# The last convolution's taps on column halves of TensorE with stacked tokens, and reordered steps in the first and third convolution and the last feed-forward part

## The reference

```python
y = conv_depthwise_3x3(x); y = y * inv + shift; return einsum('bchw,oc->bohw', y, w_pw)
...
diag = (q * k).sum(-1) * SCALE
m0_sum = diag.sum()
ktv = einsum('bnd,bne->bde', k, v)
out = m0_sum * v + SCALE * einsum('bnd,bde->bne', q, ktv) - diag[..., None] * v
```

## Time and profile before

| | |
|---|---|
| median of 3 runs | 1213.68 us (1210.94 to 1234.04) |
| the profiled execution | 1208.81 us, span 1207.0 us |
| mean granted TensorE clock | 0.952 |
| TensorE busy | 1111.6 us, 92% |
| VectorE busy | 810.0 us, 67% |
| ScalarE busy | 485.6 us, 40% |
| GpSimd busy | 255.7 us, 21% |

### The profile page before, as it was taken

One profiled execution on the slowest core, in us unless ns is written; L12 is line 12 of the kernel. 1 busy time (PEld: TensorE's weight loads), 2 busy tenths in 40 slices (PEclk: granted clock), 3 DMA queues, 4 the chain that ended last, 5 costly groups with the idle time before them and its releaser, 6 DMA issues. The chain is left out here.

```text
span 1207.0 us, 24782 instructions
## 1 busy us (share of the span) xinstructions
PE 1111.6 (92%) x8774; PEld 967.2 (80%) x8774; DVE 810.0 (67%) x2904; ACT 485.6 (40%) x976; POOL 255.7 (21%) x244
## 2 busy tenths in 40 slices
PE   3979999989999999999998988889999999999776
PEld 3758999978899998899997666568999987887554
DVE  7257676756766664577776767655877767776775
ACT  3843433425555553343342324233343422332451
POOL 5013212110211000212122534342121221211110
PEclk9979999988999999899999789899999999999887
DMA  4302010010000000000001121200000000000001
GB/s 148 95 5 69 22 47 5 0 53 1 2 2 2 1 2 1 1 2 1 0 0 36 37 48 25 49 1 1 2 1 0 0 1 1 2 1 1 5 10 40
DMA packets 15246, 21.60 MB, mean 18 GB/s; under 512 B 8761, under 2 KB 10383, under 8 KB 15026
## 3 DMA queue, kind: packets, MB, share of 16 engines
q1 hardware_dynamic: 14434, 18.53, 5.2%
q10 hardware_dynamic: 720, 1.85, 0.4%
HBM read 11.59 MB, written 3.15 MB: 12 GB/s over the span
## 5 line engine op out<-in xcount | busy, mean ns | idle before, releaser
L1222 PEld LDWEIGHTS moe_dn<-all_w,moe_hid 128*128 128x128 f32 x2304 | 269.7, 192 | 6.8 <-DVEq L1116 1.5
L1222 PE MATMUL moe_dn<-all_w,moe_hid 128*128 128x96 f32 x2304 | 271.9, 275 | 1.1 <-DVEq L1116 1.1
L1163 ACT ACTIVATE moe_hid<-moe_up 128x512 f32<-128x512 f32 x288 | 169.5, 598 | 234.5 <-PE moe_up L1214 221.4
L1212 PE MATMUL moe_up<-front_xh,front_w1h 97*128 97x512 f32 x288 | 122.1, 424 | 0.6 <-PEq L1708 0.3
L1113 DVE SCALAR_TENSOR_TENSOR all_X<-moe_dn,front_gate,all_X 128x96 f32 (+1 forms) x384 | 95.3, 311 | 29.0 <-PE moe_dn L1222 23.0
L1214 PE MATMUL moe_up<-front_xl,front_w1h 97*128 97x512 f32 x288 | 113.8, 395 | 0.0
L1213 PE MATMUL moe_up<-front_xh,front_w1l 97*128 97x512 f32 x288 | 113.4, 394 | 0.0
L1105 DVE SCALAR_TENSOR_TENSOR all_X<-all_b,front_gate,all_X 128x96 f32 (+1 forms) x384 | 98.9, 319 | 5.7 <-DVE front_var L83 2.6
L1060 POOL TENSOR_TENSOR front_prob<-front_euler,front_logit 128x16 f32<-128x16 f32 x21 | 60.9, 2900 | 193.9 <-DVEq L533 193.9
L1603 PE MATMUL l1c_o<-second_vs,l1c_pt 128*128 128x64 f32 x768 | 92.8, 274 | 0.4 <-DVE l1c_ro L1413 0.4
L1603 PEld LDWEIGHTS l1c_o<-second_vs,l1c_pt 128*128 128x128 f32 x768 | 90.2, 192 | 2.7 <-issue 0.6
(11 more groups left out here) (419 smaller groups left out, 1979.9 us busy)
## 6 DMA issues: line engine op xcount, KB each, us to landing
third_st<-third_xp SPq DMA_DIRECT2D x72, 76.5 KB, 2.1
all_w<-w SPq DMA_DIRECT2D x3, 582.0 KB
all_w<-w SPq DMA_DIRECT2D x3, 576.0 KB
all_X<-x_rows SPq DMA_DIRECT2D x2, 768.0 KB, 7.1
conv_scratch<-all_X SPq DMA_DIRECT2D x2, 768.0 KB, 3.2
all_X<-conv_scratch SPq DMA_DIRECT2D x2, 768.0 KB, 4.9
out_tokens<-l3f_y SPq DMA_DIRECT2D x5, 288.0 KB, 2.1
l0c_band<-band ACTq DMA_DIRECT2D x1, 1344.0 KB, 9.7
```

The source lines that it names most:

```text
L1163: act.activation(hid[:, n, :], up[n % UPS][:, :], ACT.Gelu).then_inc(hid_done, 1)
L1212: pe.matmul(bank, w1h[:, n, :], xh[:, p, :], start=True, stop=False)
L1222: last = pe.matmul(dn[e % 2][:, j * C:(j + 1) * C], hid[:, n, j * P:(j + 1) * P], w2[:, n, :], start=(k == 0), stop=(k == KC - 1))
```

## The change

- First convolution: `turn` makes only the lower half for groups 4 to 11; the upper half is a shifted copy of it, which SyncE moves by one transfer per group, for which `conv_piece` waits. Behind each such transfer SyncE issues an eighth of the late weights; only the first expert's and the two quantised weights still go ahead of them. One of the four instructions of `fill` goes to VectorE.
- Third convolution: on VectorE `values_out` goes ahead of `offset_norm` and one tap, and `sampled_out` ahead of the last tap; on TensorE `project(p, 0)` moves behind the next pair's offsets' taps, and the next one of `scores` ahead of `project(p, 1)`.
- Last convolution: SyncE stacks the tokens as in the third. The depthwise taps of queries and keys with values are made together by 12 matmuls with 96 x 64 weights (32 channels of either kind), two groups of channels on one column half each and the third group split by image rows over both. ScalarE and VectorE copy the results with four small instructions each; a pointwise product makes the queries. The shift of keys and values becomes row 97 of their product. The order of the calls changes, and group 1's term, statistics and variances move ahead of the barrier.
- Last feed-forward part: group 1 is normalised and turned at once, its first products go ahead of group 0's second ones, the sums of later groups go into the waits of `factors`, and a `stay_awake` of 24 stands before the last group's second products.

```diff
+            flat = xt[:, :, :, :].rearrange("p g i r -> p (g i r)")
...
+            sp.wait_ge(pads, 2)
+            for n in range(count):
+                g = TWICE + n
+                sp.wait_ge(xt_done, g + 1)
+                sp.dma_start(flat[UPPER, each * g:each * (g + 1) - 1], flat[LOWER, each * g + 1:each * (g + 1)]
+                             ).then_inc(shifted[n % 2], 16)
+                load_late(sp, T, A, size * n // count, size * (n + 1) // count)
...
-                for k in range(HC):
+                for k in range(HC if g < FIRST else HC - 1):
...
-                act.activation(x[LOWER, :, 1:SIDE + 1], image[LOWER, :, :], ACT.Copy)
-                act.activation(x[UPPER, :, 0:SIDE], image[UPPER, :, :], ACT.Copy).then_inc(xt_done, 1)
+                last = act.activation(x[LOWER, :, 1:SIDE + 1], image[LOWER, :, :], ACT.Copy)
+                if g < TWICE:
+                    last = act.activation(x[UPPER, :, 0:SIDE], image[UPPER, :, :], ACT.Copy)
+                last.then_inc(xt_done, 1)
...
+            def fill_last(g):
+                if g >= RF:
+                    dve.wait_ge(conv_done, g - RF + 1)
+                k = HC - 1
+                dve.tensor_scalar(full[:, g % RF, :, :, k, :].rearrange("p a j x -> p (a j) x"),
+                                  band[:, 2 * g:2 * g + 2, :, :].rearrange("p a j x -> p (a j) x"), own[:, k:k + 1],
+                                  None, ALU.mult).then_inc(last_done, 1)
+
+            dve.wait_ge(band_done, 2)
             for n in range(NP):
+                if n + 3 < NG:
+                    fill_last(n + 3)
...
-                        for rows in (LOWER, UPPER):
+                        for rows in (LOWER, UPPER) if g < TWICE else (LOWER,):
...
+                if g >= FIRST:
+                    pe.wait_ge(last_done, g - FIRST + 1)
+                if g >= TWICE:
+                    pe.wait_ge(shifted[(g - TWICE) % 2], 16 * ((g - TWICE) // 2 + 1))
...
+    def stack(self, sp, b, stacked):
+        for g in range(SG):
+            for r in range(KS):
+                sp.dma_start(self.st[DH * r:DH * (r + 1), b % 2, g, :, :],
+                             self.xp[DH * g:DH * (g + 1), b % 2, r:r + SIDE, :]).then_inc(stacked, 16)
+
+    def sp_tokens(self, sp):
+        sp.wait_ge(self.padded, 1)
+        self.stack(sp, 0, self.T["stacked3"][0])
...
-                    value_taps(p, 5, 6)
-                    offset_norm(p)
                 if live(p - 1):
                     values_out(p - 1)
+                if live(p):
+                    offset_norm(p)
+                    value_taps(p, 5, 6)
...
-                    value_taps(p, 6, TAPS)
+                    value_taps(p, 6, 8)
                 if live(p - 1):
                     sampled_out(p - 1, 0)
+                if live(p):
+                    value_taps(p, 8, TAPS)
...
                 if live(p - 2):
+                    project(p - 2, 0)
+                if live(p - 1):
+                    scores(p - 1, 0)
+                if live(p - 2):
                     project(p - 2, 1)
                 if live(p - 1):
-                    scores(p - 1, 0)
                     scores(p - 1, 1)
...
-                    project(p - 1, 0)
+            project(NP - 1, 0)
...
+        def places(kind):
...
+            for half in range(2):
+                rows = slice(HALF * half + DH * kind, HALF * half + DH * (kind + 1))
+                yield rows, slice(0, PIX), slice(DH * half, DH * (half + 1)), slice(0, PIX)
+                yield rows, slice(PIX, PIX + HP), slice(2 * DH, C), slice(HP * half, HP * (half + 1))
...
+        def _(sp):
+            for b in range(1, NI):
+                wait(sp, S["xp_done"], b + 1)
+                wait(sp, S["conv_in"], b - 1)
+                B.stack(sp, b, stacked[b % 2])
...
-                wait(dve, S["tap_done"], b + 1)
...
+            def kv_taps_out(b):
+                wait(dve, S["conv_in"], b + 1)
+                wait(dve, S["kv_in"], b - 1)
+                for rows, cols, chans, pixels in places(1):
+                    ins = dve.tensor_copy(ykv[chans, b % 2, pixels], qp[rows, cols])
                 ins.then_inc(S["ykv_done"], 1)
...
-                if live(st + 3) and st + 3 > 1:
-                    ln_apply(st + 3)
+                if live(st + 4):
+                    ln_apply(st + 4)
                 if live(st):
                     diagonal(st)
                 if live(st + 1):
-                    conv_kv(st + 1)
+                    kv_taps_out(st + 1)
...
-            dve.wait_ge(S["y_out"], NI)
-            add_m0(NT - 2, NT)
             add_m0(TG, 2 * TG)
+            for n in range(TG, 2 * TG):
+                last = dve.bn_stats(N["stats"][:, n, :], X[:, n, :])
+            chain.sync(last)
+            variances(dve, chain, N, TG, 2 * TG)
+            dve.tensor_scalar(N["shift"][:, TG:2 * TG], N["mean"][:, TG:2 * TG], -1.0, None, ALU.mult
+                              ).then_inc(S["first_var"], 1)
             dve.wait_ge(S["first_rstd"], 1)
             for n in range(TG):
                 normalise_tile(dve, N, N["xn"][:, 0, n, :], X, n)
+            dve.wait_ge(S["y_out"], NI)
+            add_m0(NT - 2, NT)
...
-                wait(act, S["xp_done"], b + 1)
...
+            def q_taps_out(b):
+                wait(act, S["conv_in"], b + 1)
+                wait(act, S["q_in"], b - 1)
+                for rows, cols, chans, pixels in places(0):
+                    ins = act.activation(yq[chans, b % 2, pixels], qp[rows, cols], ACT.Copy)
+                ins.then_inc(S["yq_done"], 1)
...
             for st in range(-2, NI + 1):
                 if live(st):
+                    queries_out(st)
                     kv_out(st)
-                if live(st + 2) and st + 2 > 0:
-                    tokens_out(st + 2)
+                if live(st + 1):
+                    q_taps_out(st + 1)
+                if live(st + 3) and st + 3 > 0:
+                    tokens_out(st + 3)
                 if live(st - 1):
                     heads_out(st - 1)
-                if live(st + 2):
-                    first_tap(st + 2)
-                if live(st + 1):
-                    queries_out(st + 1)
...
-            def conv_q(b):
...
+            def conv(b):
+                wait(pe, stacked[b % 2], EACH * (b // 2 + 1))
+                wait(pe, S["yq_done"], b)
+                wait(pe, S["ykv_done"], b)
+                for third in range(2):
+                    for dx in range(KS):
+                        for half in range(2):
+                            g = 2 if third else half
+                            cols, lines = ((slice(PIX, PIX + HP), slice(SIDE // 2 * half, SIDE // 2 * (half + 1)))
+                                           if third else (slice(0, PIX), slice(0, SIDE)))
+                            o = qp[HALF * half:HALF * (half + 1), cols].rearrange("c (y x) -> c y x", x=SIDE)
+                            ins = pe.matmul(o, wst[:, g, dx, :, :].rearrange("p k m -> p (k m)"),
+                                            sx[:, b % 2, g, lines, dx:dx + SIDE], start=(dx == 0), stop=(dx == KS - 1))
+                ins.then_inc(S["conv_in"], 1)
+
+            def queries(b):
+                wait(pe, S["yq_done"], b + 1)
                 wait(pe, S["q_out"], b)
-                o = qp[:, 0:PIX].rearrange("c (y x) -> c y x", x=SIDE)
-                for t in range(TAPS):
-                    dy, dx = t // KS, t % KS
-                    ins = pe.matmul(o, wqt[:, t, :], xp[:, b % 2, dy:dy + SIDE, dx:dx + SIDE],
-                                    start=(t == 0), stop=(t == TAPS - 1))
-                ins.then_inc(S["q_in"], 1)
+                wait(pe, S["zt_out"], b - 1)
+                pe.matmul(pw, wq[:, :], yq[:, b % 2, :], start=True, stop=True).then_inc(S["q_in"], 1)
...
+                wait(pe, S["q_out"], min(b + 2, NI))
...
+            pe.matmul(pp[0:1, 0:VW], shift[:, 1:2], wkv[0:C, :], start=True, stop=True).then_inc(S["row_in"], 1)
             for st in range(-2, NI + 1):
                 if live(st):
+                    queries(st)
                     keys_values(st)
-                if live(st + 2) and st + 2 > 0:
-                    turn(st + 2)
+                if live(st + 1):
+                    conv(st + 1)
+                if live(st + 3) and st + 3 > 0:
+                    turn(st + 3)
+                if live(st - 1):
+                    heads(st - 1)
                 if live(st):
                     turn_queries(st)
-                if live(st - 1):
-                    heads(st - 1)
-                if live(st + 1):
-                    conv_q(st + 1)
-                if live(st):
                     keys_by_values(st)
...
+            def last_term(g):
+                lo, hi = TG * g, TG * (g + 1)
+                chain.sync(dve.scalar_tensor_tensor(out=X[:, lo:hi, :], in0=kv[:, lo:hi, VW], scalar=m0[:, 0:1],
```

(49 more changed lines are left out.)

135 lines of the change are left out of this document (76 added, 59 removed).

## The result

The changed kernel takes 1.0075 of the kernel before (95% interval 1.0048 to 1.0101), medians 1218.99 and 1210.64 us over 20 runs each: some 9 us slower, where I had forecast 15 us faster. Its profiled execution took 1216.74 us, span 1214.6, against 1208.81 and 1207.0.

A forecast was written before the change was run, and what follows sets the result against it. TensorE was taken to bound the last convolution, VectorE close behind. Last convolution -6, third -9, first +3.5 and feed-forward -3.4 gave -15 us: 1208.8 to 1193.8 profiled, 1199 us in proportion to the median; range 1180 to 1215.

The forecast's parts named there:

- Landing takes 2.1: First convolution: group 4's shifted copy lands 2.1 us after issue, so its taps start near 42.2, not 40.09.
- are hidden: First convolution: later shifts have 3.8 us against about 3.0 needed; if that fails, each costs under 1 us.
- 14 matmuls per half: First convolution before the change: 14 matmuls per column half stream 1456 columns in 2.60 us, so halves overlap.
- 1.05 us per pair: Third convolution: the new orders save 1.05 us per pair of images, 7.4 us over 7 pairs.
- fewer waits should give some of it back: Third convolution: granted clock partly recovers, nothing to 1.3 us per pair; 1.6 us taken in all.
- The chain of five links: Last convolution: taps, transposes with heads, product and reduction, copies, and keys product set 7.15 us per image, against 7.70.
- The start: Last convolution: image 1's transfers make TensorE wait about 2.6 us; no gain there, and 2 us charged for the clock.
- B: Rival: the clock falls in the last convolution, image about 8.1 us, +14, 1213 us; chance 0.11.
- C: Rival: in the last convolution the halves run one behind the other, 2.1 us more per image, 1230 us; chance 0.04.
- D: Rival: SyncE's transfers become the last convolution's bound, 10.8 us per image at 1.2 us each, 1253 us; chance 0.04.
- A: Rival: the clock stays at full; third convolution gives 18, first costs 1.5, last gives 8; 1186 us; chance 0.24.
- at their maximum the balance is -0.2: Last feed-forward part: first clip comes 3.1 us later, but by the second group's products' maximum the balance is -0.2 us.

The follow-up runs named there:

- e1: Changed kernel with the 97-row load of l3_w1 issued as 96 rows and 1 row; ratio 0.999 to the kernel before.
- e10: Changed kernel with every 97-row load over 2 KB (experts' first weights, l3_w1) split into 96 rows and 1; ratio 0.999 to the kernel before.
- e3: Changed kernel with VectorE's and TensorE's orders in the third convolution as before; ratio 1.010 to the kernel before.
- e6: Changed kernel with six groups turned twice, VectorE's copies ahead of the diagonal, and the feed-forward edit undone; ratio 0.975 to the kernel before.

## Why the prediction was wrong

**First convolution, the step that failed by 6 us:** "Landing takes 2.1". The issue at 39.72 was right (39.74), and the clock did fall behind the wait, though that cost 1.5 us (54.20 - 48.74 against 44.03 - 40.09) and not 3.3. But I took the landing from transfers with empty queues, and had cited the page of the Trainium skill that puts 97 rows on one engine for the hold of SyncE alone. The transfer behind it had a share that came only after those rows, and landed after 8.75 us. e1, where group 4 started 3.2 us after the issue, gives the term that I had forecast: 95.3 - 92.2 = +3.1 against +3.5. The Trainium skill ("DMA: Bandwidth & Descriptors", section "Why a DMA increments its semaphore by 16 and not by 1") says that the engines used are the lowest-numbered ones, so one-engine loads and spread ones share the first; the four late packets agree. That later shifts "are hidden" held in the changed kernel by luck: the second took 8.96 us, and group 5 was late enough itself. In e10, with group 4 on time, it cost 1.25 us. The turn for one half, priced at 0.1 us less, saved nothing (1.03 us against 1.04). The "14 matmuls per half" of the pricing are 14 passes of seven matmuls; the 1456 columns are right.

**Third convolution, the term that failed by 9:** the clock. 1.05 us per pair, 7.4 for seven, was right at full clock (18.41 - 17.43 = 0.98); at equal clock e3 gives 4.5 in all. I added 1.6 us because "fewer waits should give some of it back"; instead the mean clock went from 0.87 to 0.82, 57 us at half clock and not 43, which is the seven microseconds. Fewer waits alone don't give clock: one wait of 2.0 to 2.5 us for `vbt` is left per full pair, where the pair of the kernel before had 0.7, 1.57 and 0.87. And one trace doesn't tell what the order does to the clock: with the same order and no passes the stage took from 151.3 us at 0.94 (e6) to 165.0 at 0.83 (e1). Why the clock falls in some pairs only stays open.

**Last convolution, one term.** The chain of five links was right, 7.58 us against 7.15: taps 2.10 (2.1), transposes, heads and result 1.56 (1.57), product and reduction 1.02 (1.0), keys product to taps 1.38 (1.29), and copies with the wait behind them 1.52 (1.2). The copies were mis-sized: 1.47 us for four, 0.29 or 0.43 each, as at the dear end that I had named at 1.5. Over 14 steps this leaves 1.7 us of gain and not 7.7. Measured are 3.0, because one image of the kernel before took 9.04 us, at full clock, with the statistics of a group on VectorE and GpSimd ahead of what its heads need; no image of the changed kernel is long in this way:

```profile
1024.04:1033.08 9.04, 7.60 (x42) 6.36 (x41) 7.43 (x26) 2.43 (x6) 4.36 (x6) 1.00 0.01 3
```

The start cost 1.6 us (from the first to the second keys product 9.31 us, 7.71 before), with a wait of 1.9 us for the stack where I had 2.6 and a clock of 0.82; I had charged 2 for the clock there, so this term held. In the experiments the same start took 8.3 to 11.2 us. Rivals B, C and D are out: clock 0.99 (A too, since the third convolution lost clock), halves side by side, transfers hidden even at 6.53 us. That the copies, not TensorE, were late was right; what I missed is that nothing obliged them to stand behind the diagonal.

**Feed-forward part, one term.** To the second group's maximum I had forecast +1.8 us and it was +5.1, part of it clock (0.78 against 0.86); from there to the last clip of the products I had -3.0 and it was -3.7; for the last group -2.2, and it was -1.8. The failed step: that behind the barrier "at their maximum the balance is -0.2", so that what normalising group 1 and both transposes cost ahead of the first product is given back. Besides, group 2's update and sums in the first wait for the scale have no term in the sum at all. The update ends at 1142.8, 0.5 us after the maxima's product, and the sums at 1144.6, 0.7 us after the scale's: both are in the chain.

The misses, 6.0 + 9 + 4.8 + 3.0 = 22.8 us, less 0.3 elsewhere, are the way from -15 to +7.6. The median of 1219 us lies 11 us above the forecast's own range and 4 above the widest that I gave, and on the other side of no change. The first and third convolution lay outside their own bounds; no rival had a loss in the first convolution over 5 us, though the queue that made it stood in the row that I cited.

## What to carry to other kernels

Price a transfer by what is queued on each DMA engine that it uses, not by the median landing of its kind: here one load of 97 rows held a small one back by 6.5 us. When a change makes a second engine late, look for an order in which its late piece doesn't wait for work that nobody needs yet: here two swapped lines were worth 14.5 us, more than the whole edit. Fill a wait with another group's work only where it ends before the wait does.

## What was not expected of the hardware

- A 64-row transfer inside SBUF landed 8.75 us after its issue with one 97-row load of 145.5 KB queued before it, the next one 8.96; the others 2.2 to 3.2, but for 4.7 behind two loads of 384 KB in e1 and e10. Splitting the 97-row loads into 96 rows and 1 brought the end of SyncE's issues ahead of the shifts from 39.6 us to 17.3.
- A copy of 32 partitions out of PSUM takes 0.43 us for 256 columns and 0.29 for 128, against 0.54 for 384 columns of 128 partitions. By these three the cost goes with the columns, an estimated 0.14 us for 128 beside some 0.15 for each copy, and not with the partitions; so four copies of 32 partitions are dear.
- A wait of 2.32 us was followed by half clock in e1, while the changed kernel's pairs with waits of 2.03 and 2.05 us kept 1.00.
- The mean clock differs from run to run of one kernel (0.933 to 0.964 in 20 runs of the changed one), and 0.01 of it goes with 7.8 us.
